# Three of four attention score rows sent through DRAM as broadcast loads instead of through TensorE

## The chip, the cores and the metric

One core of one Trainium2 chip runs the whole kernel. The metric is the device time of one execution in microseconds (us); lower is better. Engines are named as in the profile: PE (TensorE matmul), PEld (its weight loads, which overlap PE), DVE (VectorE), ACT (ScalarE), POOL (GpSimd), SP (SyncE, which here only issues DMAs).

## The reference

A graph of 1250 nodes and 20000 edges (plus a loop on each node) goes through two graph attention layers, a residual and a layer norm. Layer 1 has 4 heads of 512 columns, layer 2 one head of 768.

```python
def _gat_layer(x, src, dst, W, a_src, a_dst, bias, concat):
    h = (x @ W).reshape(N, H, C)
    al_s = jnp.einsum('nhc,hc->nh', h, a_src)
    al_d = jnp.einsum('nhc,hc->nh', h, a_dst)
    e = jax.nn.leaky_relu(al_s[src] + al_d[dst], NEG_SLOPE)
    m = jax.ops.segment_max(e, dst, num_segments=N)
    ex = jnp.exp(e - m[dst])
    denom = jax.ops.segment_sum(ex, dst, num_segments=N)
    alpha = ex / (denom[dst] + 1e-16)
    msg = h[src] * alpha[:, :, None]
    out = jax.ops.segment_sum(msg, dst, num_segments=N)
    out = out.reshape(N, H * C) if concat else out.mean(axis=1)
    return out + bias
h = jax.nn.elu(_gat_layer(x, src, dst, W1, att_src1, att_dst1, b1, concat=True))
out = _gat_layer(h, src, dst, W2, att_src2, att_dst2, b2, concat=False)
x = _layernorm(x + out)
```

## The kernel before

The nodes are cut into NB = 10 blocks of B = 125. The edges are first turned into a dense matrix of edge counts C (125 partitions x 10 blocks x 1250 sources), so that attention becomes dense work: for a block of 125 destinations, the scores against all 1250 sources are one tile of 125 x 1250 (`prow`), which is weighted by the counts, transposed by PE and multiplied with h.

A score is al_s[source] + al_d[destination]. The destination's part is a column (one number per partition). The source's part must stand as a row of 1250 numbers on each of 125 partitions: that is `arow`, one such tile for each head. Head h lies in slot H-1-h, so head 0 is in the last slot. The other three slots lie over `xa`, the transposed input, and may be written only when the h blocks of head 0 are done (`mm_done` reaches NB).

The four rows are made in the middle of the prologue. `score_rows` gives `rows` (8 x 1250: four source rows, four destination rows, on 8 partitions); ten small transposes (L1330) and an ACT copy (L763) turn it into columns `al`. Then `spread` (L1302) makes one head's `arow`: ten matmuls, each with a column of `al` broadcast as the stationary operand and the identity as the moving one, so that PSUM gets the row on all 125 partitions, and `row_out` (L731, L732) copies it out in two ACT instructions. Head 0 is spread first, then PE makes the last two h blocks (8 and 9), then it spreads heads 1, 2 and 3 through two sets of PSUM banks, waiting on ACT's copies.

After that comes the first attention work. For each destination block g the stages are: ACT adds the two score parts with a relu (L414), POOL adds the row again (L419, the two together are the leaky relu), DVE finds the maximum of the neighbours (`dve_max`, L437 to L449), ACT takes the exponential (L425), DVE weights by the counts (`dve_counts`, L456 to L462, signals `pc_done`), PE transposes the tile in ten pieces (`pe_transpose`, L476, signals `t_done`), ACT and DVE split the result in two parts (`act_split` L430 and L432, `dve_split` L466 and L468, the latter signals `pt_lo`), and PE multiplies (L1243 to L1245, 30 matmuls, signals `mm_done`). DVE then makes `vbuf` from PSUM, the reciprocal of the denominator and the bias (L1099), ACT and DVE apply the elu, and SP stores the block.

What orders the work: each engine's program is written out by hand, each runs strictly in its own order, and semaphores tie them. The maxima run 4 blocks ahead of the matmul, the counts 3, the splits 2. PE's step g holds: transposes of block g+1 (which wait for the counts of g+1 and for `pt_lo` of g), then the 30 matmuls of g. DVE's step g holds: wait for the matmul of g, vbuf(g), maxima of g+4, counts of g+3, split of g+2, elu of g.

All DMAs are issued by SP on one queue, in program order. Around the change: `load_w1(1)`, a wait for `rows_ps` and for `mm_done` NB (L523, L524), the load of the bias row `b1row` (125 x 2048, the same 8192 bytes to each partition, L525), three loads of `xr` (the transposed x that head 1's h blocks read, L531), and then the stores of head 0's results. DVE waits for `b1row` (semaphore `ld_b1`) once, just ahead of its first vbuf.

Of the kernel before, what the change touches and what calls it, by code (L numbers as in the profile page):

```python
# [14 lines left out]
F32 = mybir.dt.float32  # L15
# [9 lines left out]
N = 1250  # L25
E = 20000
B = 125
NB = N // B
PAIRS = E // (2 * B)
D = 768  # L30
H = 4
# [65 lines left out]
def gat_kernel(nc, x, src, dst, W1, as1, ad1, b1, W2, as2, ad2, b2, out):  # L97

    xT_d = nc.dram_tensor("xT_scratch", (NB, 128, 2, KD * B), F32, kind="Internal").ap()
    hid_d = nc.dram_tensor("hidden_scratch", (N, HID), F32, kind="Internal").ap()  # L100

    with ExitStack() as ctx:
        def sem(name):
            return ctx.enter_context(nc.semaphore(name))
# [163 lines left out]
        xT_stored = sem("xT_stored")  # L268
        ld_b1 = sem("ld_b1")
        ld_xr = [sem(f"ld_xr{i}") for i in range(XR)]  # L270
        hid_stored = [sem(f"hid_stored{i}") for i in range(2)]
# [210 lines left out]
        def _(sp):  # L482
# [39 lines left out]

            sp.wait_ge(rows_ps, 3)  # L523
            sp.wait_ge(mm_done, NB)  # L524
            sp.dma_start(b1row[:], b1.rearrange("(o n) -> o n", o=1).broadcast_to([B, HID])).then_inc(ld_b1, 16)  # L525

# [154 lines left out]
        def _(act):  # L681
# [84 lines left out]
            def scores(h, b, s):  # L766
                act_relu(act, s, prow, arow[:, H - 1 - h, :], al_up[:, h, bass.ds(b, 1)])
# [12 lines left out]
            for j in range(HB, NB):  # L780
                split_h(0, j, j % 2)
            for h in range(1, H):
                act.wait_ge(bc_ps, h + 1)
                row_out(arow[:, H - 1 - h, :], h % 2).then_inc(bc_sb, 1)
            act_split(act, 0, 0, PThi)
# [18 lines left out]
            for h in range(H):  # L804
                def step(j, s):
# [26 lines left out]
                    if more(4) and not last:  # L832
                        act.wait_ge(t_done, g + 3)
                        scores(nxt(4)[0], nxt(4)[1], s)

# [88 lines left out]
        def _(dve):  # L924
# [156 lines left out]
            dve_split(dve, 1, 1, PThi, PTlo)  # L1081
            dve.wait_ge(bc_sb, H)
            dve.wait_ge(ld_b1, 16)
# [8 lines left out]
            for h in range(H):  # L1092
                def step(j, s):
# [7 lines left out]
                    if h == 0 and not isinstance(j, int):  # L1101
                        maxima(0, j + 4)
                    if h + 1 < H and isinstance(j, int) and 6 <= j < 9:
                        maxima(h + 1, j - 6)
# [109 lines left out]
        def _(pe):  # L1214
# [120 lines left out]
            for j in range(HB, NB):  # L1335
                h_block(j)
            for h in range(1, H):
                if h >= 2:
                    pe.wait_ge(bc_sb, h - 1)
                spread(lambda b: al[:, h, b:b + 1], h % 2).then_inc(bc_ps, 1)  # L1340


            pe.wait_ge(bc_sb, 3)
            pe.wait_ge(pc_done, 1)
# [135 lines left out]
```

## Time and profile before

| | |
|---|---|
| median of 3 runs | 1033.69 us (1031.19 to 1034.45) |
| the profiled execution's own time | 1031.99 us |
| its span, first to last instruction | 1030.2 us |
| PE busy | 913.7 us, 89% of the span |
| DVE busy | 619.3 us, 60% |
| ACT busy | 401.3 us, 39% |
| POOL busy | 210.1 us, 20% |
| mean granted TensorE clock | 0.963 |
| DMA traffic | 86.65 MB, mean 84 GB/s |

Times inside the trace count from the start of the span. The stretch that the change touches lies between 185 and 240 us: it is the one place, apart from the very start and the change of layers, where PE is not nearly full. An entry in a timeline gives start, duration, engine, line, operation and, in square brackets, how long the engine sat idle before it and what ended that. A DMA share of 1.00 means that all 16 DMA engines of the core were busy.

### The profile page before, as it was taken

To read this page: it belongs to the slowest core of one execution; us is meant where nothing else is said; L and a number is where in the kernel's file an instruction comes from. 1 tells how busy PE (TensorE), PEld (TensorE's weight loads), DVE (VectorE), ACT (ScalarE), POOL (GpSimd) and SP (SyncE) were. 2 spreads that over 40 slices of the span, in tenths; PEclk is the share of its full clock that TensorE was granted. 3 is DMA by queue.
4 is the path that set the end of the run, shared out by engine and by line. 5 is a ranking of instruction groups with operands and counts; after the bars stand their busy time and mean duration, and the time that the engine had idled before them with its cause. 6 is when DMAs were issued, how large, how long until landed. Compare 5 with 4: busy or idle time off the path is not lost.

```text
span 1030.2 us, 13905 instructions
## 1 busy us (share of the span) xinstructions
PE 913.7 (89%) x4740; PEld 786.4 (76%) x4740; DVE 619.3 (60%) x1305; ACT 401.3 (39%) x574; POOL 210.1 (20%) x113
## 2 busy tenths in 40 slices
PE   0676788979999999999999999979999998479996
PEld 0454566668787788878887788869999998479995
DVE  9666568379987456863578645443221222988874
ACT  6454531256651366514663155542111112622220
POOL 1002000225530145202442023410000000343432
PEclk9987999989999999999999999989999999689998
DMA  6009975040115410263003431252111100101122
GB/s 155 1 7 191 150 227 171 7 128 27 32 32 191 179 31 29 66 219 126 30 30 102 138 103 37 93 191 111 58 63 40 74 6 1 44 21 57 59 64 69
DMA packets 38710, 86.65 MB, mean 84 GB/s; under 512 B 17251, under 2 KB 17411, under 8 KB 37032
## 3 DMA queue, kind: packets, MB, share of 16 engines
q1 hardware_dynamic: 38663, 86.04, 29.1%
q8 instruction: 28, 0.46, 0.2%
q14 instruction: 19, 0.16, 0.1%
HBM read 64.27 MB, written 21.76 MB: 84 GB/s over the span
## 4 chain that ended last, share of the span: by engine, by line
issue 38%; PE 27%; DVE 10%; ACT 8%; POOL 8%; SPq 4%; DMA 4%; DVEq 0%; POOLq 0%; ACTq 0%
PE ps L1243 7%; PE ps L1245 7%; PE ps L1244 7%; POOL prow L419 5%; SPq L501 4%; DVE junk_w L1032 2%; POOL W1lo L629 2%; PE ps L1353 2%; DMA hidden_scratch<-ebuf 2%; DMA xT_scratch<-xa 1%; PE ps L1274 1%; ACT prow L414 1%; DVE nbr L437 1%; DVE prow L456 1%; ACT oh_lo L701 1%
## 5 line engine op out<-in xcount | busy, mean ns | idle before, releaser
L419 POOL TENSOR_TENSOR prow<-prow,arow 125x1250 f32<-125x1250 f32 x50 | 139.3, 2789 | 633.4 <-ACT prow L414 633.4
L1243 PE MATMUL ps<-hhi,PThi 125*125 125x512 f32 x400 | 162.2, 405 | 1.0 <-DVE hlo L1019 1.0
L1244 PE MATMUL ps<-hlo,PThi 125*125 125x512 f32 x400 | 158.5, 396 | 0.0
L1245 PE MATMUL ps<-hhi,PTlo 125*125 125x512 f32 x400 | 158.1, 395 | 0.0
L425 ACT ACTIVATE prow<-prow,expb 125x1250 f32<-125x1250 f32 x50 | 67.0, 1340 | 172.7 <-POOL prow L419 151.5
L1243 PE MATMUL ps<-W2p,hT 128*125 128x384 f32 x320 | 110.6, 346 | 6.7 <-DVE W2p L1129 5.6
L1245 PE MATMUL ps<-W2p,hT 128*125 128x384 f32 x320 | 108.7, 340 | 0.0
L1244 PE MATMUL ps<-W2p,hT 128*125 128x384 f32 x320 | 108.5, 339 | 0.0
L1088 DVE TENSOR_TENSOR hT<-ps,hT 128x500 fp32r<-128x500 f32 x40 | 25.3, 674 | 128.4 <-ACT hT L797 124.0
L476 PE MATMUL ps<-ident,prow 125*125 125x125 f32 x500 | 68.1, 286 | 28.4 <-DVE prow L456 12.2
L476 PEld LDWEIGHTS ps<-ident,prow 125*125 125x125 f32 x500 | 65.0, 199 | 35.0 <-issue 30.6
L456 DVE SCALAR_TENSOR_TENSOR prow<-prow,counts 125x1250 f32<-125x1250 f32 x50 | 74.4, 1488 | 26.1 <-ACT prow L425 25.3
L1245 PEld LDWEIGHTS ps<-hhi,PTlo 125*125 125x125 f32 x400 | 74.6, 187 | 19.4
L1243 PEld LDWEIGHTS ps<-hhi,PThi 125*125 125x125 f32 x400 | 74.7, 187 | 18.6 <-DVE hlo L1019 1.5
L1244 PEld LDWEIGHTS ps<-hlo,PThi 125*125 125x125 f32 x400 | 74.6, 186 | 17.0
L441 DVE CUSTOM_DVE_ANT_0 nbr<-nbr,arow 125x1250 bf16<-125x1250 bf16 x50 | 77.3, 1546 | 2.1
L1046 DVE TENSOR_SCALAR ring<-table,ekey 125x420 bf16<-125x420 uint16 (+1 forms) x210 | 56.0, 341 | 34.5 <-issue 11.7
L694 ACT ACTIVATE hhi<-ps 125x512 fp32r<-125x512 f32 (+1 forms) x40 | 23.8, 597 | 134.9 <-PE ps L1245 134.9
L1243 PE MATMUL ps<-W1hi,xr 128*125 128x512 f32 x180 | 71.2, 396 | 2.1 <-DMA xr<-xT_scratch 2.1
L797 ACT ACTIVATE hT<-ps 128x500 fp32r<-128x500 f32 x40 | 21.3, 584 | 132.2 <-PE ps L1353 132.2
L1099 DVE SCALAR_TENSOR_TENSOR vbuf<-ps,rden,b1row 125x512 f32<-125x512 f32 x40 | 29.8, 746 | 69.1 <-PE ps L1245 69.1
L1244 PE MATMUL ps<-W1lo,xr 128*125 128x512 f32 x180 | 71.1, 395 | 0.0
(157 smaller groups left out, 1818.2 us busy)
## 6 DMA issues: line engine op xcount, KB each, us to landing
xr<-xT_scratch SPq DMA_DIRECT2D x30, 750.0 KB, 4.4
hidden_scratch<-ebuf SPq DMA_DIRECT2D x40, 250.0 KB
hblk<-hidden_scratch SPq DMA_DIRECT2D x10, 1000.0 KB
xT_scratch<-xa SPq DMA_DIRECT2D x20, 375.0 KB, 13.2
w1raw<-in_L_gnn_W SPq DMA_DIRECT2D x4, 1536.0 KB, 7.7
w1raw<-in_L_gnn_W SPq DMA_DIRECT2D x12, 512.0 KB, 3.6
w2late<-in_L_gnn_W SPq DMA_DIRECT2D x10, 384.0 KB, 8.0
xres<-in_x SPq DMA_DIRECT2D x10, 375.0 KB
```

What stands on the lines that cost most here:

```text
L419: pool.tensor_tensor(buf[:, s, :], buf[:, s, :], row, ALU.add).then_inc(e_done, 1)
L425: act.activation(buf[:, s, :], buf[:, s, :], ACT.Exp, scale=SLOPE, bias=expb[:, bass.ds(g, 1)]).then_inc(p_done, 1)
L441: dve.tensor_tensor_reduce(out=scr[:], in0=scr[:], in1=row, scale=1.0, scalar=-3.0e38, op0=ALU.add, op1=ALU.max, accum_out=mx[:]).then_inc ...
L456: dve.scalar_tensor_tensor(buf[:, s, :], buf[:, s, :], 1.0, C[:, bass.ds(b, 1), :].rearrange("p o n -> p (o n)"), ALU.min, ALU.mult, accum ...
L476: t = pe.transpose(PS[0:B, 2 + bank, (b - lo) * B:(b - lo + 1) * B], buf[:, s, b * B:(b + 1) * B], ident[0:B, 0:B])
L501: sp.dma_start(xT_d[j, :, u, :].rearrange("p (k n) -> p k n", k=KD), xa[:, u, :, j, :].bitcast(F32)).then_inc(xT_stored, 16)
L1046: oh = dve.tensor_scalar(ring[:, w % 2, v, 0:win_cols(w)], table[:, w % TR, 0:win_cols(w)], ekey[:, bass.ds(at_slot(first, i, v), 1)], Non ...
L1088: lo = dve.tensor_tensor(ht_part(half, 1, a), PS[:, bank, 0:4 * B], ht_part(half, 0, a).bitcast(F32), ALU.subtract)
L1099: dve.scalar_tensor_tensor(vbuf[:, s, :], PS[0:B, s, :], rden[:, bass.ds(g, 1)], b1row[:, h * HC:(h + 1) * HC], ALU.mult, ALU.add).then_in ...
L1243: pe.matmul(dst, ahi, bhi, start=start, stop=False)
L1244: pe.matmul(dst, ahi, blo, start=False, stop=False)
L1245: return pe.matmul(dst, alo, bhi, start=False, stop=stop)
```

## The change

The rows of heads 1 to 3 are no longer spread by PE. SP stores the three rows of `rows` (on partitions 1 to 3) into a scratch tensor in DRAM as soon as ACT has written them, waits for that store, waits for `mm_done` NB as before, and issues three loads, one for each head, that read one row of 5000 bytes 125 times and put it on 125 partitions. They stand in SP's queue ahead of the load of `b1row`. The three spreads of PE and the six copies of ACT go away. ACT and DVE wait for the loads where they first touch head 1's row, late in head 0. DVE's wait for all four `bc_sb` before its first vbuf goes; its wait for `ld_b1` stays.

```diff
+    rows_d = nc.dram_tensor("rows_scratch", (H - 1, N), F32, kind="Internal").ap()
...
-            sp.wait_ge(rows_ps, 3)
+            sp.wait_ge(rows_sb, 3)
+            sp.dma_start(rows_d[:, :], rows[1:H, :]).then_inc(rows_stored, 16)
+            sp.wait_ge(rows_stored, 16)
             sp.wait_ge(mm_done, NB)
+            for h in range(1, H):
+                sp.dma_start(arow[:, H - 1 - h, :], rows_d[h - 1, :].rearrange("(o n) -> o n", o=1).broadcast_to([B, N])
+                             ).then_inc(ld_arow, 16)
             sp.dma_start(b1row[:], b1.rearrange("(o n) -> o n", o=1).broadcast_to([B, HID])).then_inc(ld_b1, 16)
...
             for j in range(HB, NB):
                 split_h(0, j, j % 2)
-            for h in range(1, H):
-                act.wait_ge(bc_ps, h + 1)
-                row_out(arow[:, H - 1 - h, :], h % 2).then_inc(bc_sb, 1)
             act_split(act, 0, 0, PThi)
...
                         act.wait_ge(t_done, g + 3)
+                        if h == 0 and isinstance(j, int) and j == NB - 4:
+                            act.wait_ge(ld_arow, 16 * (H - 1))
                         scores(nxt(4)[0], nxt(4)[1], s)
...
             dve_split(dve, 1, 1, PThi, PTlo)
-            dve.wait_ge(bc_sb, H)
             dve.wait_ge(ld_b1, 16)
...
+                    if h == 0 and isinstance(j, int) and j == 6:
+                        dve.wait_ge(ld_arow, 16 * (H - 1))
                     if h + 1 < H and isinstance(j, int) and 6 <= j < 9:
                         maxima(h + 1, j - 6)
...
             for j in range(HB, NB):
                 h_block(j)
-            for h in range(1, H):
-                if h >= 2:
-                    pe.wait_ge(bc_sb, h - 1)
-                spread(lambda b: al[:, h, b:b + 1], h % 2).then_inc(bc_ps, 1)
-
-
-            pe.wait_ge(bc_sb, 3)
+            pe.wait_ge(bc_sb, 1)
             pe.wait_ge(pc_done, 1)
             pe_transpose(pe, 0, 0, prow)
```

On PE, at the end of the h blocks of head 0, this stood before (the last rows of h block 9, the three spreads, and the first two `pe_transpose`):

```order
L1244 MATMUL ps<-W1lo,xa 125x512
L1245 MATMUL ps<-W1hi,xa 125x512
L1302 MATMUL ps<-ident,al 125x125 x10
L1302 MATMUL ps<-ident,al 125x125 [waits bc_sb]
L1302 MATMUL ps<-ident,al 125x125 x9
L1302 MATMUL ps<-ident,al 125x125 [waits bc_sb]
L1302 MATMUL ps<-ident,al 125x125 x9
L476 MATMUL ps<-ident,prow 125x125 [waits pc_done,bc_sb]
L476 MATMUL ps<-ident,prow 125x125 x9
L476 MATMUL ps<-ident,prow 125x125 [waits pt_lo,pc_done]
L476 MATMUL ps<-ident,prow 125x125 x9
```

The same place of the changed kernel (its line numbers are a few higher) is this:

```order
L1252 MATMUL ps<-W1lo,xa 125x512
L1253 MATMUL ps<-W1hi,xa 125x512
L479 MATMUL ps<-ident,prow 125x125 [waits pc_done,bc_sb]
L479 MATMUL ps<-ident,prow 125x125 x9
L479 MATMUL ps<-ident,prow 125x125 [waits pt_lo,pc_done]
L479 MATMUL ps<-ident,prow 125x125 x9
```

Thirty matmuls and two waits on ACT's copies are gone, and the transposes of block 0 follow h block 9 directly, with their own wait for `pc_done`.

On SP, after the twelve loads of W1 pieces, this stood before:

```order
L516 DMA w1raw<-in_L_gnn_W 128x1024 [waits wa_done] x9
L492 DMA w1raw<-in_L_gnn_W 128x6x512 [waits wa_done]
L525 DMA b1row<-in_L_gnn_b 125x2048 [waits mm_done,rows_ps]
L531 DMA xr<-xT_scratch 128x1500 x3
L77 UNCONDITIONAL_BRANCH
```

And this stands there now:

```order
L519 DMA w1raw<-in_L_gnn_W 128x1024 [waits wa_done] x9
L495 DMA w1raw<-in_L_gnn_W 128x6x512 [waits wa_done]
L527 DMA rows_scratch<-rows 3x1250 [waits rows_sb]
L531 DMA arow<-rows_scratch 125x1250 [waits mm_done,rows_stored]
L531 DMA arow<-rows_scratch 125x1250 x2
L533 DMA b1row<-in_L_gnn_b 125x2048
L539 DMA xr<-xT_scratch 128x1500 x3
L77 UNCONDITIONAL_BRANCH
```

One small store and three loads of 125 x 1250 came in ahead of `b1row` and `xr`; nothing else on SP moved.

## Rows read from the trace of the kernel before

**Rows 1.** The page: busy time of each engine, and the chain's shares

```profile
PE 913.7 (89%) x4740; PEld 786.4 (76%) x4740; DVE 619.3 (60%) x1305; ACT 401.3 (39%) x574; POOL 210.1 (20%) x113
issue 38%; PE 27%; DVE 10%; ACT 8%; POOL 8%; SPq 4%; DMA 4%; DVEq 0%; POOLq 0%; ACTq 0%
```

**Rows 2.** Timeline of PE's weight loads, 203 to 250 us (start, duration, what, idle before)

```profile
204.02 4.57 PEld L1302 LDWEIGHTS ps<-ident,al 125*125 125x125 f32 x40
210.90 2.26 PEld L1302 LDWEIGHTS ps<-ident,al 125*125 125x125 f32 x20 [2.31 <-ACT arow L732]
213.07 1.17 PEld L476 LDWEIGHTS ps<-ident,prow 125*125 125x125 f32 x10
218.06 2.17 PEld L476 LDWEIGHTS ps<-ident,prow 125*125 125x125 f32 x10 [3.81 <-issue]
...
237.20 1.29 PEld L476 LDWEIGHTS ps<-ident,prow 125*125 125x125 f32 x10
```

**Rows 3.** Timeline of DVE, 203 to 250 us

```profile
210.44 1.45 DVE L456 SCALAR_TENSOR_TENSOR prow<-prow,counts 125x1250 f32<-125x1250 f32 x1
211.81 0.08 DVE L456 DVE_READ_ACCUMULATOR prow<-prow,counts 125x1 f32 x1
...
216.42 1.20 DVE L466 TENSOR_TENSOR PTlo<-ps,PThi 125x1000 fp32r<-125x1000 f32 x1
217.53 0.41 DVE L468 TENSOR_TENSOR PTlo<-ps,PThi 125x250 fp32r<-125x250 f32 x1
...
228.74 0.41 DVE L468 TENSOR_TENSOR PTlo<-ps,PThi 125x250 fp32r<-125x250 f32 x1
229.39 0.75 DVE L1099 SCALAR_TENSOR_TENSOR vbuf<-ps,rden,b1row 125x512 f32<-125x512 f32 x1 [0.24 <-PE ps L1245]
...
236.26 0.41 DVE L468 TENSOR_TENSOR PTlo<-ps,PThi 125x250 fp32r<-125x250 f32 x1
```

**Rows 4.** Timeline of ACT, 203 to 250 us

```profile
214.28 0.37 ACT L732 ACTIVATE arow<-ps 125x250 f32<-125x250 f32 x1
214.54 1.01 ACT L430 ACTIVATE PThi<-ps 125x1000 fp32r<-125x1000 f32 x1
215.42 0.40 ACT L432 ACTIVATE PThi<-ps 125x250 fp32r<-125x250 f32 x1
...
220.56 1.00 ACT L430 ACTIVATE PThi<-ps 125x1000 fp32r<-125x1000 f32 x1 [3.52 <-PE ps L476]
```

**Rows 5.** Timeline of SP's DMA issues, 170 to 320 us

```profile
204.49 0.29 SPq L525 DMA_DIRECT2D b1row<-in_L_gnn_b  x1
204.82 1.27 SPq L531 DMA_DIRECT2D xr<-xT_scratch  x3
238.14 71.65 SPq L535 DMA_DIRECT2D hidden_scratch<-ebuf  x10
309.84 6.58 SPq L531 DMA_DIRECT2D xr<-xT_scratch  x3
```

**Rows 6.** Windows of 2 us; the last three columns: granted clock, DMA share, GB/s

```profile
204.00:206.00 2.00, 2.00 (x19) 1.93 (x18) 1.92 (x5) 1.11 (x1) 0.58 (x1) 1.00 0.25 26
...
208.00:210.00 2.00, 0.78 (x8) 0.59 (x6) 0.77 (x2) 2.00 (x4) 0.00 (x0) 1.00 1.03 250
212.00:214.00 2.00, 2.00 (x21) 2.00 (x20) 1.90 (x7) 0.63 (x2) 0.00 (x0) 1.00 0.98 222
214.00:216.00 2.00, 0.43 (x4) 0.24 (x3) 1.92 (x6) 2.00 (x5) 0.00 (x0) 1.00 1.05 237
216.00:218.00 2.00, 0.00 (x0) 0.00 (x0) 1.93 (x6) 1.04 (x1) 0.88 (x1) 0.78 0.44 119
220.00:222.00 2.00, 2.00 (x7) 1.64 (x7) 1.84 (x5) 1.44 (x3) 0.00 (x0) 0.50 0.33 135
222.00:224.00 2.00, 2.00 (x6) 1.58 (x5) 0.00 (x0) 2.00 (x2) 0.86 (x1) 0.51 0.30 126
224.00:226.00 2.00, 2.00 (x10) 1.57 (x10) 1.68 (x1) 0.28 (x1) 2.00 (x1) 1.00 0.01 3
```

**Rows 7.** DMA packets of 218 to 219 and of 219 to 226 us

```profile
DMA packets 24, 0.13 MB, mean 127 GB/s; under 512 B 5, under 2 KB 5, under 8 KB 18
DMA packets 123, 0.66 MB, mean 94 GB/s; under 512 B 15, under 2 KB 15, under 8 KB 122
```

**Rows 8.** The load hblk (125 x 2048) alone: packets of 798 to 808 us, and windows

```profile
DMA packets 130, 1.02 MB, mean 102 GB/s; under 512 B 5, under 2 KB 5, under 8 KB 5
800.00:805.00 5.00, 5.00 (x31) 5.00 (x30) 1.52 (x4) 0.00 (x0) 0.00 (x0) 1.00 0.31 131
805.00:810.00 5.00, 5.00 (x34) 4.97 (x33) 1.26 (x2) 1.07 (x2) 0.00 (x0) 1.00 0.11 46
```

**Rows 9.** Timeline of DVE and of POOL, 201 to 205 us

```profile
201.80 2.80 DVE L446 SCALAR_TENSOR_TENSOR negm<-mneg 125x1 f32<-125x1 f32 x1
206.93 0.16 DVE L446 SCALAR_TENSOR_TENSOR negm<-mneg 125x1 f32<-125x1 f32 x1
...
201.71 2.87 POOL L419 TENSOR_TENSOR prow<-prow,arow 125x1250 f32<-125x1250 f32 x1
```

More of the change, by code:

```diff
@@ L269, in gat_kernel @@
         ld_b1 = sem("ld_b1")
+        rows_stored = sem("rows_stored")
+        ld_arow = sem("ld_arow")
         ld_xr = [sem(f"ld_xr{i}") for i in range(XR)]
```

## The prediction

> **What bounds the kernel now.** I read the page first. PE is busy for 89% of the span, no other engine for more than 60%, and PE's share of the chain is the largest of any engine [rows 1]. So time is lost or won only where PE stands still, or where it runs at the lower clock. The changed stretch is such a place, and there I read the timeline of PE's weight loads [rows 2]. PE does the spreads of heads 1 and 2 from 204.02 to about 208.6, waits 2.31 us for ACT's copy, does the spread of head 3 from 210.90, and goes straight on to the transposes of block 0 at 213.07, which take 1.17 us. Then it stands for 3.81 us, and does the transposes of block 1 at 218.06 in 2.17 us, nearly twice the time for the same ten pieces. The windows say why: the granted clock is 1.00 up to 216, 0.78 from 216 to 218, 0.50 and 0.51 up to 224, then 1.00 again [rows 6]. A gap of 3.81 us thus ended with TensorE at 1.2 GHz instead of 2.4, for about 5.9 us after PE had started again.
>
> What ends the gap at 218.06 is read on DVE: the split of block 0, L466 and L468, ends at 217.94 [rows 3]. DVE comes to it in its own order (counts 0, counts 1, maxima 2, split 0), from 210.44 on. From 220 to 285 us PE and DVE both run nearly without a pause, DVE a little ahead: its split for block 2 ends at 236.67 [rows 3], and PE comes to the transposes that need it at 237.20 [rows 2]. DVE's lead is 0.5 us, no more.
>
> **What goes away.** Three spreads of PE and three pairs of copies of ACT. PE's work is 4.57 + 2.26 = 6.8 us, and with the wait between them the stretch from 204.02 to 213.07 is 9.05 us [rows 2]. This isn't the gain. The transposes of block 0 also wait for `pc_done` 1, the counts of block 0. DVE writes it at 211.89 [rows 3], behind work that the change doesn't touch. PE can therefore start the transposes at about 212.05, 1.0 us sooner. That is the most the removal can bring, and I cost it at nothing, for two reasons. First, PE would by then have stood from about 204.1 to 212.05, 7.9 us, twice the gap after which the clock was found at 0.50. At that clock the same transposes take 2.50 us from their start until ACT can evict (218.06 to 220.56), where at full clock it was 1.47 us (213.07 to 214.54) [rows 2, 4]. 212.05 + 2.50 = 214.55, against 214.54 before. Second, even 1.0 us less there ends at DVE: ACT's two parts are done at 215.82 [rows 4] and DVE comes to split 0 only at 216.42 [rows 3]. The cover is DVE's own queue. With that cover gone, the 1.0 us would be the gain.
>
> ACT's six copies go too, but the last ends at 214.65 and ACT then waits for the same transposes [rows 4], so nothing behind them comes sooner. The clock in the stretch from 218 to 224 is low before and, after a longer gap, low again: no difference.
>
> **What comes in.** The store of three rows starts at about 192, when the rows are written, and SP would otherwise wait until 204.49 [rows 5]. Twelve microseconds cover it. The three loads are the real cost. They aren't needed until late in head 0, beyond 280 us, but they stand in the queue ahead of `b1row`, and DVE waits for `b1row` before its first vbuf, with maxima 4, counts 3 and split 2 queued behind it.
>
> How long does a load onto 125 partitions take? The load hblk (125 rows of 8192 bytes) runs alone from 798: the DMA share is 0.31 and the rate 131 GB/s [rows 8]. 0.31 is 5 of 16: such a load runs on five DMA engines. `b1row` has the same shape and bytes, and what is left over after 217 shows it too: share 0.33 and 0.30, 135 and 126 GB/s [rows 6]. I take `arow`, also 125 rows, to be the same.
>
> `b1row` was issued at 204.49 [rows 5]. Its packets are the ones of 8192 bytes: between 218 and 219 six packets are of that size or more (24 less 18), after 219 one single packet [rows 7]. So it landed at about 218.7. That is 14.2 us after its issue, where 1.02 MB at 131 GB/s make 7.8, because from 207 to 216 all sixteen engines were busy with `xr` too and together moved only 222 to 250 GB/s [rows 6], 75 for the five.
>
> The new loads put 3 x 625 kB = 1.875 MB on the same five engines ahead of it. The slow stretch with `xr` lasts as long as before (the eleven other engines have the same `xr` bytes), so all that is added runs at 131 GB/s: 14.3 us. `b1row` then lands at 218.7 + 14.3 = 233.0. DVE wants it at 229.15, when split 1 is done, and its vbuf started at 229.39 [rows 3]. It would start at 233.1, 3.7 us later. Behind it split 2 ends at 240.4, and PE, which comes at 237.2, can start its transposes at 240.5: **3.3 us** lost. Nothing gives it back, since PE and DVE run without slack from there.
>
> The bounds of the landing. From below: the slow stretch might not come back, since no row says what made it. Data begin to move some 1.5 us after the issue (only 26 GB/s from 204 to 206 [rows 6]), and 2.90 MB at 131 GB/s take 22.1 us: landing at 228.1, a microsecond before it is wanted, cost nothing. From above: the five engines might stay at 75 GB/s: 38.7 us, landing at about 244.7, vbuf 15.4 us late, cost 14.9. I take 233.0, because it uses each rate in the stretch where the trace shows it.
>
> The Trainium skill, "DMA: Bandwidth & Descriptors", section Specifications, gives about 27 GiB/s (29 GB/s) for one engine. By that figure five engines would move the 2.90 MB in about 20 us and `b1row` would be in time. The trace has 26 GB/s an engine when five run alone and 15 when sixteen do, so here the row and the page part, and the row decides. The same page ("Why a DMA increments its semaphore by 16 and not by 1") says that the number of engines is the largest up to 16 that divides the outermost sizes, which for 125 is 5; the share of 0.31 agrees.
>
> **The clock behind the new gap.** PE would stand from 237.2 to 240.5, 3.3 us; the gap of 3.81 us ended in the low clock [rows 2], the gap of 2.31 us did not (1.00 from 212 to 216 [rows 6]). 3.3 lies between, nearer to the upper one. If the clock falls, about 5.9 us run at half speed, 2.9 us lost (from 0 to 2.9). I take 2.9.
>
> **The sum.** 0 for the removal, 3.3 for the stall, 2.9 for the clock: 6.2 us. The profiled execution took 1031.99 us in all (its span is 1030.2), so 1038.2. The median of the runs is 1033.69, 1.7 us above the profiled one, so runs of one kernel differ by more than some terms of this sum. I leave 1038.2 and widen the range. No difference of under about 0.3% (3.1 us) can be told from no change.
>
> One thing disturbs each of these numbers by up to some 2 us either way: where POOL's add runs, some small DVE instructions wait for its end. L446 took 2.80 us beside a POOL add of 2.87, and 0.16 without it [rows 9]. A shift of ACT against DVE changes which ones are hit.
>
> **The rivals.**
> The loads are hidden anyway: `b1row` lands by 229. For it: the lower bound of the landing. Against it: the 222 to 250 GB/s in three windows [rows 6]. Time 1032 to 1034.5. Chance 0.24.
> The stall comes, but the clock holds: 1031.99 + 3.3 = 1035.3, up to 1036.8 with POOL in the way. For it: the gap of 2.31 us. Chance 0.19.
> DMA is slower still: equal row read 375 times, five engines at 75 GB/s all the time: 1031.99 + 14.9 = 1046.9 at the far end. Nothing in the profile speaks for it but that the slow stretch is unexplained. Chance 0.06.
> Faster: the clock. If PE started the transposes at 212 at full clock and the low stretch up to 224 didn't come, its 5.9 us at half speed would give back 2.9 us, and with 1.0 from the earlier start the time would be 1028.1. It needs PE to do something between 204 and 212, or the gap not to count; it decides only if `b1row` lands before about 230. Against it: 7.9 us is the longest gap in this stretch. Chance 0.06.
> My forecast, the stall and the clock, has 0.45: 1036.8 to 1041.
>
> **How the numbers follow.** Faster 0.06. Same: 0.24 + 0.19 = 0.43. Slower: 0.45 + 0.06 = 0.51. The range: 1031.8 (hidden loads) to 1041.5 (forecast with POOL in the way) leaves out the fast clock, the very slow DMA, and a little at either edge.
>
> **What would show it.** In the trace after: the first `pe_transpose` at about 212 with the clock at 0.50; the DMA share near 0.31 from about 217.5 to past 233; DVE idle before its first vbuf for some 4 us, put down to the DMA of `b1row`; PE's transposes of block 3 at about 240.5 after an idle of 3 us, and a low clock after it. If DVE isn't idle before vbuf, the loads are hidden and I am wrong; if the windows from 207 to 216 show 400 GB/s, the rate was the wrong step; if the clock is 1.00 after 240, the last term falls.

## The result, and the profile after

The changed kernel takes 1039.63 us (median of 7 runs, 1039.04 to 1040.93), against 1033.69 us (7 runs, 1031.19 to 1036.7) of the kernel before on the same chip. The ratio is 1.0066, with a 95% interval of 1.0050 to 1.0081: slower by 6.8 us (5.2 to 8.4). Predicted were 1038.2 us, with a range of 1031.8 to 1041.5. The profiled execution took 1040.05 us, its span is 1037.9 us, its mean granted clock 0.955. Ratios, here and below, are formed from executions in the fast state alone; one slow execution of experiment 10 (1542 us at a mean clock of 0.56) is left out of its ratio.

The page, engines: busy time, share of the span, instructions (before: [rows 1]).

```profile
PE 912.5 (88%) x4680; PEld 784.8 (76%) x4680; DVE 619.8 (60%) x1305; ACT 398.3 (38%) x568; POOL 210.8 (20%) x113
```

PE has 60 instructions fewer (each of the thirty matmuls of the spreads shows as two in the trace) and is busy for 1.2 us less, ACT for 3.0 us less, and yet the span is 7.7 us longer. So work isn't what has grown; waiting is.

One correction comes first. SP's first load of the changed place starts at 206.44, against 204.49 before, and both wait there for the same last h block. Of these 1.95 us, 1.46 are there long before the changed place: the issue of `w1raw` that is at 75.15 before is at 76.61 after. In the other executions shown below that first load starts anywhere from 204.81 to 209.55, and at 205.46 and 209.55 in two variants of the kernel before (experiments 10 and 8) that move nothing ahead of it. I take this for a difference between executions, and compare by "before's clock": times of a trace less the amount by which its first load behind `mm_done` is late. From that load to the end of the span it is 825.7 us before and 831.5 after: **5.8 us**, where the prediction's terms make 6.2.

The timeline of PE's weight loads after (start, duration, what, idle before; the four groups of transposes of blocks 0 to 3), beside [rows 2]:

```profile
213.98 2.17 PEld L479 LDWEIGHTS ps<-ident,prow 125*125 125x125 f32 x10 [8.06 <-issue]
220.03 2.17 PEld L479 LDWEIGHTS ps<-ident,prow 125*125 125x125 f32 x10 [3.88 <-issue]
...
231.25 1.17 PEld L479 LDWEIGHTS ps<-ident,prow 125*125 125x125 f32 x10 [1.07 <-issue]
...
242.69 2.17 PEld L479 LDWEIGHTS ps<-ident,prow 125*125 125x125 f32 x10 [3.56 <-DVE PTlo L471]
```

Blocks 2, 4 and 5 before, which [rows 2] leaves out:

```profile
229.26 1.17 PEld L476 LDWEIGHTS ps<-ident,prow 125*125 125x125 f32 x10 [0.56 <-issue]
...
245.25 1.29 PEld L476 LDWEIGHTS ps<-ident,prow 125*125 125x125 f32 x10
...
253.96 1.17 PEld L476 LDWEIGHTS ps<-ident,prow 125*125 125x125 f32 x10 [0.68 <-DVE PTlo L468]
```

On before's clock the four start at 212.03, 218.08, 229.30 and 240.74. The first comes 1.04 us sooner than before and takes 2.17 us where it took 1.17; the second is where it was (218.06). The third is in time for the old schedule (229.26). The fourth is 3.54 us later than 237.20, and at 2.17 us it is a slow one again. What it waited for is the split on DVE, so DVE's timeline is next, beside [rows 3]:

```profile
218.40 1.19 DVE L469 TENSOR_TENSOR PTlo<-ps,PThi 125x1000 fp32r<-125x1000 f32 x1
219.51 0.41 DVE L471 TENSOR_TENSOR PTlo<-ps,PThi 125x250 fp32r<-125x250 f32 x1
...
230.73 0.41 DVE L471 TENSOR_TENSOR PTlo<-ps,PThi 125x250 fp32r<-125x250 f32 x1
235.72 0.75 DVE L1105 SCALAR_TENSOR_TENSOR vbuf<-ps,rden,b1row 125x512 f32<-125x512 f32 x1 [4.58 <-DMA b1row<-in_L_gnn_b]
```

DVE finishes split 1 at 231.14 and then stands for 4.58 us until `b1row` has landed; before, the idle time at this place was 0.24 us and PE ended it. The queue that `b1row` came through is in SP's timeline, beside [rows 5]:

```profile
193.99 0.27 SPq L527 DMA_DIRECT2D rows_scratch<-rows  x1
206.44 1.05 SPq L531 DMA_DIRECT2D arow<-rows_scratch  x3
207.53 0.34 SPq L533 DMA_DIRECT2D b1row<-in_L_gnn_b  x1
207.92 7.86 SPq L539 DMA_DIRECT2D xr<-xT_scratch  x3
```

The load of `b1row` is issued only 1.1 us behind the first `arow`. So the time went into the transfer, not into issuing. The windows after, beside [rows 6] (us, busy time of PE, PEld, DVE, ACT and POOL with counts, granted clock, DMA share, GB/s):

```profile
212.00:214.00 2.00, 0.00 (x0) 0.02 (x1) 1.97 (x4) 0.00 (x0) 0.00 (x0) 0.50 0.68 135
214.00:216.00 2.00, 1.99 (x9) 2.00 (x10) 1.90 (x7) 0.00 (x0) 0.00 (x0) 0.50 0.76 253
218.00:220.00 2.00, 0.00 (x0) 0.00 (x0) 1.93 (x6) 0.98 (x1) 0.94 (x1) 0.50 1.00 237
222.00:224.00 2.00, 2.00 (x8) 1.60 (x7) 1.79 (x5) 1.47 (x3) 0.00 (x0) 0.50 0.92 214
224.00:226.00 2.00, 2.00 (x8) 1.62 (x7) 0.00 (x0) 2.00 (x2) 0.89 (x1) 0.77 0.32 118
232.00:234.00 2.00, 2.00 (x13) 1.71 (x12) 0.00 (x0) 1.27 (x2) 0.00 (x0) 1.00 0.32 135
242.00:244.00 2.00, 1.31 (x6) 1.31 (x7) 2.00 (x4) 0.99 (x1) 2.00 (x2) 0.50 0.00 0
246.00:248.00 2.00, 2.00 (x7) 1.50 (x6) 1.59 (x6) 1.97 (x5) 0.00 (x0) 0.50 0.17 66
248.00:250.00 2.00, 2.00 (x9) 1.55 (x8) 1.84 (x5) 1.46 (x2) 0.47 (x1) 0.80 0.00 0
```

Two things are to be seen. The DMA share is 0.32 and the rate 118 to 135 GB/s from 224 to past 234: five engines alone work off the queue. And a second stretch of low clock stands from 242 to 249, behind the new gap of PE; before, the clock is 1.00 in all windows there, and its ten transposes at 237.20 took 1.29 us.

When `b1row` landed is read from the sizes of the packets. Its own are of 8192 bytes, those of `arow` and `xr` are smaller. Here are 233 to 234 and 235 to 236 us of after:

```profile
DMA packets 16, 0.13 MB, mean 131 GB/s; under 512 B 0, under 2 KB 0, under 8 KB 0
DMA packets 23, 0.14 MB, mean 138 GB/s; under 512 B 0, under 2 KB 0, under 8 KB 23
```

At 233 every packet is one of `b1row`, at 235 none. In between five of 24 are at least that large, so it landed at about 235, on before's clock 233.1.

### The profile page after: what moved, and what is told of

Read it like the earlier page. It is cut to its first block, busy times and chain, and to the rows that moved or that the text cites. A ratio compares the mean times of both kernels' runs of the same rounds, so it can differ in the third digit from the quotient of the medians.

```text
span 1037.9 us, 13783 instructions
## 1 busy us (share of the span) xinstructions
PE 912.5 (88%) x4680; PEld 784.8 (76%) x4680; DVE 619.8 (60%) x1305; ACT 398.3 (38%) x568; POOL 210.8 (20%) x113
## 4 chain that ended last, share of the span: by engine, by line
issue 38%; PE 27%; DVE 10%; ACT 8%; POOL 8%; SPq 4%; DMA 4%; DVEq 0%; POOLq 0%; ACTq 0%
PE ps L1251 7%; PE ps L1253 7%; PE ps L1252 7%; POOL prow L422 5%; SPq L504 4%; DVE junk_w L1039 2%; POOL W1lo L637 2%; PE ps L1355 2%; DMA hidden_scratch<-ebuf 2%; DMA xT_scratch<-xa 1%; PE ps L1282 1%; ACT prow L417 1%; DVE prow L459 1%; PE ps L479 1%; DVE nbr L440 1%
## 5 line engine op out<-in xcount | busy, mean ns | idle before, releaser
L479 PE MATMUL ps<-ident,prow 125*125 125x125 f32 x500 | 70.3, 292 | 39.1 <-DVE prow L459 19.8
L479 PEld LDWEIGHTS ps<-ident,prow 125*125 125x125 f32 x500 | 67.1, 205 | 46.2 <-issue 39.0
```

The source lines that it names most:

```text
L479: t = pe.transpose(PS[0:B, 2 + bank, (b - lo) * B:(b - lo + 1) * B], buf[:, s, b * B:(b + 1) * B], ident[0:B, 0:B])
```

## The experiments

What was to be told apart: that the loads ahead of `b1row` delay it and that PE's gap then costs clock too (my theory); that the new traffic as such costs, wherever it stands (rival A); that the missing spreads cost, since PE now stands cold before the first transposes (rival B); and that the clock behind the new gap is worth nothing. Each experiment is measured against the kernel before on its own chip, in executions of both taken beside each other. These chips gave 1035.23, 1035.12 and 1033.87 us for it, so ratios are compared, not times. "In the trace" is the time from the first load behind `mm_done` to the end of the span, less before's 825.7; it is read from one execution of each kernel.

**1. The bias row goes first.** Nothing else is changed.

```diff
+            sp.dma_start(b1row[:], b1.rearrange("(o n) -> o n", o=1).broadcast_to([B, HID])).then_inc(ld_b1, 16)
             for h in range(1, H):
                 sp.dma_start(arow[:, H - 1 - h, :], ...).then_inc(ld_arow, 16)
-            sp.dma_start(b1row[:], b1.rearrange("(o n) -> o n", o=1).broadcast_to([B, HID])).then_inc(ld_b1, 16)
```

> The changed kernel with one difference: the load of b1row stands ahead of the three arow loads in SP's queue, not behind them. Theory (queue): the loss is b1row's late landing and the low clock behind it; here b1row lands about 16 us earlier, near 219 or sooner, DVE doesn't wait for it, PE's transposes of block 3 follow at once at full clock. Time as before, 1033.7 us, within 2 us; ratio to before 1.000. Rival A (traffic): the 1.9 MB of broadcast loads beside the compute costs by itself, wherever it stands: 1039 to 1040. Rival B (removal): the longer gap of PE from 204 to 212 and its low clock cost the time: 1039 to 1040 too, with DVE not idle before its first vbuf. Rival C: the removal brings its 1 us after all: 1032.7.

Measured: 1036.21 us, ratio 1.0015 (1.0002 to 1.0028); in the trace +0.8 us. DVE and PE of this run, from its timelines:

```profile
229.41 0.74 DVE L1105 SCALAR_TENSOR_TENSOR vbuf<-ps,rden,b1row 125x512 f32<-125x512 f32 x1
...
212.35 2.18 PEld L479 LDWEIGHTS ps<-ident,prow 125*125 125x125 f32 x10 [8.06 <-issue]
218.40 2.17 PEld L479 LDWEIGHTS ps<-ident,prow 125*125 125x125 f32 x10 [3.88 <-issue]
...
237.55 1.29 PEld L479 LDWEIGHTS ps<-ident,prow 125*125 125x125 f32 x10
```

No idle time ahead of vbuf, and the transposes of block 3 at 237.23 on before's clock, at full speed. The 8 us of standing and the slow first transposes are as in the changed kernel, and the same bytes are moved. So some five of the 6.8 us (1.0066 less 1.0015; with both intervals, 3 to 7) hang on the order of the loads alone. Rivals A and B can hold no more than what is left, 1.5 us (0.2 to 2.9).

**2. Two rows ahead of the bias row, one behind.** This asks whether the loss grows with each load or sets in at a point.

```diff
-            for h in range(1, H):
+            for h in range(1, 3):
                 sp.dma_start(arow[:, H - 1 - h, :], ...).then_inc(ld_arow, 16)
             sp.dma_start(b1row[:], ...).then_inc(ld_b1, 16)
+            for h in range(3, H):
+                sp.dma_start(arow[:, H - 1 - h, :], ...).then_inc(ld_arow, 16)
```

> The changed kernel with the loads of heads 1 and 2 ahead of b1row and that of head 3 behind it. Theory (queue): 1.25 MB on five engines at 131 GB/s are ahead, 9.5 us, so b1row lands at about 228.3 by the clock of the trace before (230 by that of the trace after, which runs 2 us later from its start on), just before DVE wants it: DVE's idle before its first vbuf is under 1 us, the time is that of before, 1033.7, at most 1035. If the cost were proportional to the bytes ahead (rival D: two thirds of the loss), 1037.6. Rivals A and B as in the kernel with b1row first: 1039 to 1040.

Measured: 1036.54 us, ratio 1.0015 (1.0000 to 1.0029); in the trace -0.7 us. DVE's vbuf starts at 231.35, on before's clock 229.06, without idle time. The packets from 229 to 230 are still of 8192 bytes but for one, from 230 to 231 all are smaller, so `b1row` landed at about 230.3, on before's clock 228.0. 625 kB less ahead of it brought it 5.1 us sooner (233.1 to 228.0), where 625 kB at 131 GB/s are 4.8. It was then a microsecond early, and the stall was gone (by the ratio 1.6 us may be left, 0.0 to 3.0): two thirds of the loads cost little or nothing, the third one costs the rest.

**3. The same loads on all the engines.** Each load of 125 partitions is cut in one of 112 and one of 13 (`XP` is 112). The order stays.

```diff
-                sp.dma_start(arow[:, H - 1 - h, :], rows_d[h - 1, :].rearrange("(o n) -> o n", o=1).broadcast_to([B, N])
-                             ).then_inc(ld_arow, 16)
+                for lo, hi in ((0, XP), (XP, B)):
+                    sp.dma_start(arow[lo:hi, H - 1 - h, :], rows_d[h - 1, :].rearrange("(o n) -> o n", o=1).broadcast_to([hi - lo, N])
+                                 ).then_inc(ld_arow, 16)
```

> The changed kernel, all three arow loads ahead of b1row as there, but each cut into a load of 112 partitions and one of 13. Theory (queue, five engines): 112 partitions go to 16 engines, so 1.875 MB take 5 to 8 us and not 14.3; b1row lands at about 224 to 227 and DVE hardly waits: 1033.7, at most 1035. In the windows behind the issue the DMA share is near 1.00 where it was 0.31. Rival E: the delay is made of bytes or of reading one DRAM row 375 times, not of the number of engines: share high or low, b1row lands at 233 or later and the time stays at 1039 to 1040.

Measured: 1033.99 us, ratio 0.9997 (0.9981 to 1.0012); in the trace -1.0 us. Windows of this run, its vbuf, and its DMA packets from 228.5 to 229 and from 229 to 230:

```profile
208.00:210.00 2.00, 0.00 (x0) 0.00 (x0) 1.84 (x5) 0.89 (x1) 0.00 (x0) 1.00 0.92 295
210.00:212.00 2.00, 0.00 (x0) 0.00 (x0) 0.10 (x1) 1.96 (x3) 0.00 (x0) 0.95 0.68 210
...
231.75 0.74 DVE L1106 SCALAR_TENSOR_TENSOR vbuf<-ps,rden,b1row 125x512 f32<-125x512 f32 x1
...
DMA packets 10, 0.06 MB, mean 124 GB/s; under 512 B 0, under 2 KB 0, under 8 KB 9
DMA packets 20, 0.11 MB, mean 108 GB/s; under 512 B 2, under 2 KB 2, under 8 KB 20
```

The share is 0.92 and 0.68 where the changed kernel has 0.31 to 0.33 in its first windows, and vbuf starts at 231.75 (229.08 on before's clock) without idle time. With every other part of the change in place the kernel is as fast as before. The bytes ahead of `b1row` still delay it: its last large packet is at 228.7, on before's clock 226.0, where it is at 218.5 before and at 232.6 in the changed kernel. But they delay it by 7.5 us and not by 14, and DVE wants it only at 229.1. So it is not the bytes alone that make the loss, but that five engines carry them.

**4. Matmuls with no use in the new gap.** The changed kernel; 13 matmuls into an unused PSUM bank behind the matmuls of block 1, so that PE isn't idle while it waits for DVE. They add work and leave out none.

```diff
+                    if h == 0 and isinstance(j, int) and j == 1:
+                        for _ in range(13):
+                            pe.matmul(PS[0:B, 6, :], hhi[:, 0, 0:B], hhi[:, 0, :], start=True, stop=True)
```

> The changed kernel with 13 matmuls of 125x512 on PE (3.0 us at full clock, results unused) behind the matmuls of block 1 of head 0, where PE stands and waits for the late DVE. The DMA queue is as in the changed kernel, so b1row is as late and DVE waits 4 to 5 us as there. Theory (stall and clock, two separate terms): the granted clock stays 1.00 through the stall, and the time falls by the clock's term alone, 2.9 us (2 to 3.3): 1036.7. If the clock cost nothing (its slow stretch hidden behind DVE): 1039.6 or 0.3 more. If the clock is the whole loss and the stall nothing: 1033.7.

Measured: 1038.27 us, ratio 1.0037 (1.0020 to 1.0053); in the trace +3.4 us. Its PEld timeline, and a window:

```profile
240.29 2.98 PEld L1380 LDWEIGHTS ps<-hhi 125*125 125x125 f32 x13
244.07 1.17 PEld L479 LDWEIGHTS ps<-ident,prow 125*125 125x125 f32 x10 [0.81 <-DVE PTlo L471]
...
244.00:246.00 2.00, 1.93 (x14) 1.79 (x15) 2.00 (x4) 1.60 (x2) 2.00 (x2) 1.00 0.02 7
```

The transposes still start 3.0 us late (240.24 on before's clock against 237.20), since DVE is as late as it was, but they take 1.17 us instead of 2.17, and the clock is 1.00. The stall is left, but for half a microsecond, and the clock is given back. The span shrinks by 2.4 us in the trace (5.8 less 3.4), and 0.5 of that is the shorter stall, so the clock's part is 1.9. By the ratios it is 3.0 (1.0066 less 1.0037), but with both intervals that means anything from 0.7 to 5.3. Predicted were 2.9. How the loss runs is seen in the changed kernel's blocks 4 and 5:

```profile
253.48 1.29 PEld L479 LDWEIGHTS ps<-ident,prow 125*125 125x125 f32 x10
...
261.55 1.29 PEld L479 LDWEIGHTS ps<-ident,prow 125*125 125x125 f32 x10
```

From block 3 to block 4 it takes 10.79 us where it was 8.05, 2.7 us more; but from block 3 to block 5 18.86 where it was 16.76, only 2.1 more. Before, PE stood for 0.68 us ahead of block 5, waiting for DVE; now it doesn't.

**5. The loads alone, in the kernel before.** The store of the rows and three loads of the same shape go in ahead of `b1row`, into an unused tile `dump`. All spreads and copies stay as they were. ACT waits for the store before it copies head 1's row, and SP waits for the loads before it fetches the first blocks of layer 1's result again, at the end of head 3.

```diff
-            sp.wait_ge(rows_ps, 3)
+            sp.wait_ge(rows_sb, 3)
+            sp.dma_start(rows_d[:, :], rows[1:H, :]).then_inc(rows_stored, 16)
+            sp.wait_ge(rows_stored, 16)
             sp.wait_ge(mm_done, NB)
+            for h in range(1, H):
+                sp.dma_start(dump[:, h - 1, :], rows_d[h - 1, :]...broadcast_to([B, N])).then_inc(ld_dump, 16)
```

> The kernel before, spreads and copies kept, with only the DMAs of the change added: the store of the three rows and three loads of 125 x 1250 ahead of b1row, into SBUF that nobody reads. Theory (queue): the added loads are the whole loss, so this kernel is as slow as the changed one, 5.8 to 6.5 us above before: ratio 1.006, DVE idle some 4.5 us before its first vbuf, PE idle 3 to 3.7 us before the transposes of block 3, low clock behind it. Rival B (removal): if the missing PE work with its longer gap had a part in the loss, this kernel is faster than the changed one by that part; if the removal had a gain that was hidden in the sum, it is slower.

Measured: 1043.22 us, ratio 1.0082 (1.0066 to 1.0097); in the trace +6.8 us. DVE and PEld:

```profile
236.85 0.75 DVE L1110 SCALAR_TENSOR_TENSOR vbuf<-ps,rden,b1row 125x512 f32<-125x512 f32 x1 [5.51 <-DMA b1row<-in_L_gnn_b]
...
215.27 1.17 PEld L480 LDWEIGHTS ps<-ident,prow 125*125 125x125 f32 x10
220.26 2.17 PEld L480 LDWEIGHTS ps<-ident,prow 125*125 125x125 f32 x10 [3.81 <-issue]
...
244.18 2.17 PEld L480 LDWEIGHTS ps<-ident,prow 125*125 125x125 f32 x10 [4.84 <-DVE PTlo L472]
```

The spreads are all there, the first transposes run at full clock as before, and the loss comes in whole: added loads alone make the changed kernel's time and a little more: 8.5 us by the ratio, where the changed kernel has 6.8 and the intervals overlap. The trace puts the surplus ahead of block 3 (DVE's idle time is 5.51 us instead of 4.58). Its last large packet of `b1row` is at 234.9, on before's clock 232.7 and so no later than in the changed kernel; why DVE went on 0.9 us later isn't told. With experiments 1 and 3 this settles the cause from both sides.

The traces also part the loss into its two terms. The first column is the time from the first load behind `mm_done` to the transposes of block 3, the second from there to the end of the span (us):

| kernel | to block 3 | from there to the end |
|---|---|---|
| before | 32.71 | 793.0 |
| changed | 36.25 | 795.2 |
| 1, bias row first | 32.74 | 793.8 |
| 2, two ahead | 32.72 | 792.3 |
| 3, split loads | 32.72 | 792.0 |
| 4, gap filled | 35.75 | 793.3 |
| 5, loads alone | 37.51 | 795.0 |

Where the stall is gone (1 to 3), block 3 is back at its old place to 0.03 us. The stall is 3.5 us, and what comes on top behind block 3 is 2.2 us in the changed kernel and 2.0 in experiment 5, the two with the low clock there: together they are the 5.8. The five others lie between 792.0 and 793.8, so this second term is known to about a microsecond.

The other six ask for the second half of the prediction: was the removal worth nothing for the reasons I gave, and could it be made worth something?

**6. Unused matmuls where the spreads were.** Kernel of experiment 3, with 32 matmuls right behind h block 9, so that the first transposes run at full clock.

```diff
+            for _ in range(32):
+                pe.matmul(PS[0:B, 6, :], hhi[:, 0, 0:B], hhi[:, 0, :], start=True, stop=True)
             pe.wait_ge(bc_sb, 1)
             pe.wait_ge(pc_done, 1)
```

> The kernel with split loads (112 and 13 partitions, b1row in time), with 32 unused matmuls of 125x512 on PE (7.4 us) right behind h block 9, so that PE reaches the transposes of block 0 at full clock. Theory (DVE's order covers it): the transposes take 1.2 us and not 2.2, ACT has its part 1.0 us sooner, and DVE still comes to split 0 at the same time; PE stands still longer before block 1 and finds the low clock there as before: same time as the kernel with split loads, within 0.5 us in the trace. Rival F: the 1.0 us is passed on: 1.0 us faster. Rival G: POOL's add now begins 1.0 us sooner, beside DVE's small instructions ahead of split 0, and holds one of them until it ends: 1 to 2.2 us slower.

Measured: 1038.57 us, ratio 1.0031 (1.0020 to 1.0042), and 3.1 us more in the trace than experiment 3 (2.1 of them by block 3). PEld, DVE and POOL:

```profile
215.72 1.17 PEld L479 LDWEIGHTS ps<-ident,prow 125*125 125x125 f32 x10 [0.60 <-issue]
223.86 2.17 PEld L479 LDWEIGHTS ps<-ident,prow 125*125 125x125 f32 x10 [6.97 <-issue]
...
219.87 2.25 DVE L449 SCALAR_TENSOR_TENSOR negm<-mneg 125x1 f32<-125x1 f32 x1
...
219.69 2.41 POOL L422 TENSOR_TENSOR prow<-prow,arow 125x1250 f32<-125x1250 f32 x1 [11.40 <-ACT prow L417]
```

The transposes are fast, ACT copies their result a microsecond sooner, and so it gives POOL its add a microsecond sooner. That add now starts 0.2 us ahead of a DVE instruction of one element, which lasts until the add ends (222.12 and 222.10), 2.25 us instead of 0.16. Split 0 stands behind it in DVE's order, and PE's next transposes behind split 0. Finishing sooner made the kernel slower.

**7. The same with 17 more between the transposes of blocks 0 and 1.**

```diff
             pe_transpose(pe, 0, 0, prow)
+            for _ in range(17):
+                pe.matmul(PS[0:B, 6, :], hhi[:, 0, 0:B], hhi[:, 0, :], start=True, stop=True)
```

> As the one before, with 17 more unused matmuls (3.9 us) between the transposes of block 0 and of block 1, so that no low clock is left between 204 and 230. PE's transposes of block 1 and the matmuls of block 0 run at full clock. Theory: PE gains 2.9 us there, but DVE sets the pace behind it (counts 2 wait for ACT's exponential, which comes 1.0 us sooner, and POOL's add holds them), so only 1.0 to 1.2 us arrive at the end: 1.0 us under the kernel with split loads. Rival: all of the clock's 2.9 us arrive. If rival G of the kernel before holds, up to 2.2 us more.

Measured: 1038.86 us, ratio 1.0034 (1.0022 to 1.0045). DVE was held as in experiment 6 (2.26 us), so PE still had a gap of 3.26 us, and the transposes of block 1 took 2.17 us behind it. What it was meant to test, the old gap at full clock, did not come about.

**8. The old gap at full clock, in the kernel before.** 14 matmuls between the transposes of blocks 0 and 1, with a wait for ACT's last copy ahead of them; nothing else.

```diff
             pe_transpose(pe, 0, 0, prow)
+            pe.wait_ge(bc_sb, H)
+            for _ in range(14):
+                pe.matmul(PS[0:B, 6, :], hhi[:, 0, 0:B], hhi[:, 0, :], start=True, stop=True)
```

> The kernel before with 14 unused matmuls (3.3 us) between the transposes of block 0 and of block 1, where it stands 3.8 us and falls to the low clock. This is what the rival that ended faster rested on. Theory: the clock stays at 1.00, PE gains 2.9 us, of which DVE passes on 1.0 to 1.2: ratio to before 0.999. If the clock's whole price counts: 0.997.

Measured: 1035.79 us, ratio 1.0002 (0.9991 to 1.0012); in the trace -0.9 us. The transposes of blocks 1 and 2:

```profile
223.15 1.17 PEld L476 LDWEIGHTS ps<-ident,prow 125*125 125x125 f32 x10 [0.26 <-issue]
...
233.26 1.17 PEld L476 LDWEIGHTS ps<-ident,prow 125*125 125x125 f32 x10 [2.18 <-issue]
```

The low stretch is gone (1.17 us where it was 2.17). But on before's clock block 2 starts at 228.20, 1.06 us sooner, and not 2.9: PE now waits 2.18 us ahead of it, since DVE isn't ready: its counts 2 begin only when ACT's exponential is done, and take 3.02 us (3.01 before). One microsecond can't be told from nothing here.

**9. Everything for the start of PE.** Kernel of experiment 3 with `b1row` first and cut in two as well, DVE's split 0 ahead of maxima 2, 32 matmuls before the first transposes and 12 behind them.

```diff
+            for lo, hi in ((0, XP), (XP, B)):
+                sp.dma_start(b1row[lo:hi, :], b1...broadcast_to([hi - lo, HID])).then_inc(ld_b1, 16)
...
-            maxima(0, 2)
             dve_split(dve, 0, 0, PThi, PTlo)
+            maxima(0, 2)
```

> A version meant to make the removal pay. As in the kernel with split loads the rows come by DMA in pieces of 112 and 13 partitions, b1row is split likewise and stands first. DVE makes split 0 ahead of the maxima of block 2, and not behind them, so that ACT's earlier part is used. PE gets 32 unused matmuls ahead of the transposes of block 0 and 12 (2.8 us) behind them, which keep its clock at 1.00. Theory: split 0 ends at 216.4 on the clock of the trace before (217.94 there), transposes of block 1 begin at 216.5 and take 1.2 us, and the transposes of block 2 begin 2 to 2.7 us sooner than before, DVE and POOL setting the pace: ratio to before 0.9975. Rival: a DVE instruction held by POOL's add takes it back: 1.000 or above.

Measured: 1035.85 us, ratio 1.0025 (1.0010 to 1.0040), a miss. PEld and DVE:

```profile
216.91 1.17 PEld L479 LDWEIGHTS ps<-ident,prow 125*125 125x125 f32 x10 [0.64 <-issue]
...
229.76 1.72 PEld L479 LDWEIGHTS ps<-ident,prow 125*125 125x125 f32 x10 [4.96 <-issue]
...
216.71 2.58 DVE L440 TENSOR_SCALAR nbr<-counts 125x1250 bf16<-125x1250 uint16 x1
...
221.03 2.75 DVE L449 SCALAR_TENSOR_TENSOR negm<-mneg 125x1 f32<-125x1 f32 x1
```

The transposes of block 1 start 1.68 us sooner on before's clock (216.38 against 218.06). Then POOL's adds hold DVE twice, the gap ahead of block 2 is 4.96 us, and block 2 starts at 229.2, where the changed kernel, with no help at all, has 229.30. All of the gain is given back, and block 3 comes at 238.77, 1.6 us later than before (237.20).

**10. DVE's new order alone, in the kernel before.**

```diff
-            maxima(0, 2)
             dve_split(dve, 0, 0, PThi, PTlo)
+            maxima(0, 2)
```

> The kernel before with the new order of DVE alone (split 0 ahead of the maxima of block 2). The spreads stay, so ACT's part of block 0 is done at 215.82, and split 0 ends at 217.5, 0.4 us sooner: same time as before within 0.5 us, ratio 0.9996. If it gains as much as the version with the rows by DMA and the filled gaps, removal and clock have no part in that gain.

Measured: 1037.15 us, ratio 1.0029 (1.0015 to 1.0043), a miss too. Two DVE instructions are held again, for 2.56 and 2.71 us, and block 2's transposes start at 231.29, on before's clock 230.32, 1.1 us later than the 229.26 of the kernel before.

**11. Experiment 9 without the unused matmuls.**

```diff
-            for _ in range(32):
-                pe.matmul(PS[0:B, 6, :], hhi[:, 0, 0:B], hhi[:, 0, :], start=True, stop=True)
...
-            for _ in range(12):
-                pe.matmul(PS[0:B, 6, :], hhi[:, 0, 0:B], hhi[:, 0, :], start=True, stop=True)
```

> As the version with new order and filled gaps, without the unused matmuls. PE stands from 204 to 212 and makes the transposes of block 0 at the low clock, so ACT's part comes at 215.8 as before. Theory (the low clock eats the removal's gain): like the kernel before with the new order, ratio 0.9996, 2 us above the version with filled gaps. If the gain of that version comes from the order alone, this one has it too: 0.9975.

Measured: 1035.04 us, ratio 1.0010 (0.9996 to 1.0023). DVE is held at `nbr` of maxima 2 (2.57 us) and at a small instruction of maxima 3 (2.71 us), as in experiment 10. No version is faster than the kernel before; the changed kernel with split loads (experiment 3) is level with it.

## Why the prediction was right

By its own steps, times on before's clock:

- **The removal, costed at 0.** Right, and for the reasons given. The first transposes were expected at 212.05 at half clock, with ACT's part at 214.55; they started at 212.03, in windows of clock 0.50, and ACT's part at 214.53. Split 0 followed at 216.45, as before (216.42). Experiment 3, where the removal stands without the stall, has block 3 at its old place. The second reason, DVE's own order, is borne out by experiment 6: ACT's part came 1.1 us sooner, and DVE was at the `negm` ahead of split 0 at 216.17 on before's clock, when it was there before (216.15). But it came out worse than I wrote: from there POOL's add held DVE, and by block 3 that was not 0 but a loss of 2.1 us. The prediction had named this as a disturbance of up to 2 us.
- **The landing of `b1row`.** Expected 233.0, read 233.1. The arithmetic was right though one of its pictures was not: the slow stretch in which all the engines share some 214 to 253 GB/s didn't begin at 207 but at about 213, 211 on before's clock, since SP needed 7.86 us instead of 1.27 for its three issues of `xr`. It was about as long, and for the five engines only its length counts. Experiment 2 gives the price of one load, 5.1 us, where 4.8 were reckoned.
- **The stall.** vbuf was expected at 233.1 and started at 233.77; the 0.7 us between landing and start weren't in the sum. PE's transposes were expected at 240.5 and came at 240.74: 3.5 us late, not 3.3.
- **The clock behind the gap.** Expected to fall, and it did, from 242 to 249. 2.9 us were taken, and that is about what PE had lost by block 4 (2.7). "Nothing gives it back" was wrong: PE had waits of 0.7 us for DVE further on that took a part of it up, and 1.9 to 2.2 us were left (experiment 4 and the table; the ratios can't tell this from 2.9).
- **The sum.** 6.2 us expected, 5.8 in the trace, 6.8 (5.2 to 8.4) by the ratio. That the sum is nearer than its terms is in part luck: the stall was 0.2 us too small and the clock 0.7 too large. The predicted 1038.2 us stood on the profiled execution, 1.7 us below the median of its kernel; that is more than the 1.4 us by which it is short.

Of the rivals, "hidden anyway" and "the stall without the clock" fall with DVE's idle 4.58 us and the windows after 242. "DMA slower still" falls with the landing. The rival on the other side, "faster by the clock", was over-priced. It gave 2.9 us for the low stretch from 218 to 224, and experiment 8 took that stretch away and got 1.06 us through, too little to tell by the ratio. The step that fails is to count time at the low clock as lost in full: the loss lasts only as far as PE is the last to come. Behind block 3 that holds for two thirds to three quarters of it, behind block 1 for little more than a third, since DVE would have kept PE waiting for the rest.

Left open: experiments 1 and 2 have a ratio of 1.0015, some 1.5 us, of which their traces show +0.8 and -0.7. It doesn't lie ahead of block 3 (32.74 and 32.72 against 32.71). Whether it belongs to the change or to the runs isn't told. Nor was it tried what makes the sixteen engines share only 240 GB/s. It isn't only the 5-engine shape: in experiment 9, with all the row loads split, they still move 263 GB/s in the mean from 211 to 218, and 402 to 444 from 219 to 223, when only packets of the size of `xr`'s are left.

## What to carry to other kernels

A transfer that isn't needed for long still costs at once if it stands in a queue ahead of one that is: add up the bytes ahead of each load that something waits for, at the rate of the engines that this shape really uses (the DMA share tells how many), and compare with the moment it is wanted. Here 125 partitions meant five engines, and one load more was the difference between a microsecond early and four late; putting the urgent load first took some five of the 6.8 us away, and cutting each in 112 and 13 partitions all of them, and in both traces the stall was gone entirely. Work that is taken off an engine is worth what the next wait leaves of it, and here that was nothing, since the engine only stood longer and came back at the lower clock.

## What the runs showed of the hardware

- **A small DVE instruction can last as long as POOL's add.** With the instructions otherwise alike, `negm` (one element for each partition) took 0.16 us, or 2.25 and 2.75 us if POOL's add had started just before it, and `nbr` (L440) 0.48 or 2.58 us. The split (L469), which reads one input from PSUM, took 1.18 to 1.20 us throughout. The Trainium skill, "SBUF — State Buffer", section Who interferes with whom, says that a DVE instruction with two inputs in SBUF contends with a POOL instruction that reads SBUF, and that the port pair they share is an exclusive lock, so that the order of issue decides who waits. The end times agree to 0.02 us in experiment 6 (222.10 and 222.12), where `negm` came second. What I hadn't expected is the consequence: a microsecond gained ahead of it can turn into two or three lost.
- **Issuing 16-engine loads took SP longer behind 5-engine loads.** The three issues of `xr` took 1.27 us behind one such load, 7.86 us behind four, 9.44 us with the same four in another order (experiment 1), 2.33 us behind three split loads and `b1row` (experiment 3), and 1.30 us with `b1row` split too (experiment 9).
- **The gaps of PE and the clock.** Transposes behind gaps of 3.25 us and more took 2.17 us, at a granted clock of 0.50, that is 1.2 GHz; behind gaps of up to 2.37 us they took 1.17 us, or up to 1.29 where there was none. One is in between: behind a gap of 4.96 us in experiment 9 they took 1.72 us, and there the granted clock was still 1.00 when they began at 229.76 and fell while they ran (0.64 from 230 to 231).
